# Second attention: running maxima taken off by marker products, and the score products of two batches interleaved by bands

## The reference

```
q, k = apply_rope(split_heads(x)), apply_rope(split_heads((x @ w_dk + b_dk) @ w_uk + b_uk))
v = split_heads((x @ w_dv + b_dv) @ w_uv + b_uv)
attn = softmax(einsum('bhid,bhjd->bhij', q, k) / sqrt(8), axis=-1)
x = layernorm(x + einsum('bhij,bhjd->bhid', attn, v).reshape(Bx, Tx, Dx) @ w_o + b_o)
```

## Time and profile before

| | |
|---|---|
| median of 3 runs | 1437.58 us (1434.99 to 1444.62) |
| the profiled execution's own time | 1433.81 us |
| its span in the profile | 1431.9 us |
| TensorE busy | 1295.6 us, 90% of the span |
| VectorE busy | 957.0 us, 67% |
| ScalarE busy | 863.9 us, 60% |
| second attention (788.4 to 1216.0 us) | 427.6 us |

### The profile page before, as it was taken

One profiled execution on the slowest core, in us unless ns is written; L12 is line 12 of the kernel. 1 busy time (PEld: TensorE's weight loads), 2 busy tenths in 40 slices (PEclk: granted clock), 3 DMA queues, 4 the chain that ended last, 5 costly groups with the idle time before them and its releaser, 6 DMA issues. The chain is left out here.

```text
span 1431.9 us, 33756 instructions
## 1 busy us (share of the span) xinstructions
PE 1295.6 (90%) x10829; PEld 1053.9 (74%) x10829; DVE 957.0 (67%) x2849; ACT 863.9 (60%) x2233; POOL 617.5 (43%) x965
## 2 busy tenths in 40 slices
PE   6999999999999999799997898898889888978877
PEld 5888888888888888799996565555555554756765
DVE  6787877777787887667775667767766753543323
ACT  4777777776777766356643555555554544846643
POOL 3244444444444444435534345444543422435553
PEclk9999999999999999899998679878877975989998
DMA  7020202020312210132131222022050002022215
GB/s 259 20 89 26 86 26 86 30 88 28 97 46 73 83 54 17 55 113 65 57 129 52 76 76 78 21 83 75 22 196 8 13 13 82 18 82 80 78 53 184
DMA packets 56451, 100.88 MB, mean 70 GB/s; under 512 B 11056, under 2 KB 46256, under 8 KB 53616
## 3 DMA queue, kind: packets, MB, share of 16 engines
q1 hardware_dynamic: 46704, 80.06, 17.5%
q0 software_dynamic: 9088, 18.89, 3.8%
q10 hardware_dynamic: 576, 0.86, 0.2%
HBM read 78.81 MB, written 62.06 MB: 98 GB/s over the span
## 5 line engine op out<-in xcount | busy, mean ns | idle before, releaser
L622 ACT ACTIVATE a_prob<-psum,a_nmx 128x128 f32<-128x128 f32 (+1 forms) x512 | 208.3, 425 | 72.8 <-DVE a_nmx L985 72.8
L855 POOL TENSOR_TENSOR a_prob<-a_prob,a_rl 128x128 f32<-128x128 f32 (+1 forms) x256 | 124.3, 507 | 241.7 <-DVE a_rl L989 241.0
L2664 DVE TENSOR_REDUCE f_nmx<-psum 128x4 f32<-128x1024 f32 x120 | 147.0, 1225 | 56.1 <-PE psum L214 52.3
L2418 ACT ACTIVATE a_prob<-psum 128x1024 f32<-128x1024 f32 x128 | 130.9, 1023 | 36.9 <-PE psum L2150 34.0
L629 ACT ACTIVATE a_probt<-psum 128x768 f32<-128x768 f32 x128 | 104.8, 819 | 79.5 <-PE psum L1432 79.5
L902 POOL DMA_INDIRECT yt<-a_yrow,a_dest x78 | 79.4, 1018 | 106.9 <-ACT a_yrow L671 89.4
L622 ACT ACTIVATION_READ_ACCUMULATOR a_prob<-psum,a_nmx 128x1 f32 x512 | 107.9, 211 | 0.0
L1432 PE MATMUL psum<-ident,a_prob 128*128 128x128 f32 x768 | 105.3, 273 | 1.1 <-DVE a_prob L995 0.7
L1789 POOL DMA_INDIRECT yt<-m_yrow,m_dest x78 | 76.1, 975 | 69.7 <-DVE m_yrow L1936 45.7
L974 DVE TENSOR_TENSOR a_qkt<-psum,a_bqk 128x512 f32<-128x512 f32 x128 | 88.2, 689 | 26.3 <-PE psum L109 23.7
L2160 PE MATMUL psum<-a_prob,a_v 128*32 128x256 f32 x1024 | 94.5, 502 | 1.4 <-DVEq L2726 1.3
(11 more groups left out here) (411 smaller groups left out, 3838.6 us busy)
## 6 DMA issues: line engine op xcount, KB each, us to landing
xs<-in_fill SPq DMA_DIRECT2D x144, 264.0 KB, 4.2
a_xrow<-xs SPq DMA_DIRECT2D x39, 132.0 KB
m_xrow<-xs SPq DMA_DIRECT2D x39, 132.0 KB
f_yin<-yt SPq DMA_DIRECT2D x18, 256.0 KB, 2.9
w<-in_w SPq DMA_DIRECT2D x16, 256.0 KB, 3.4
f_yin<-yt SPq DMA_DIRECT2D x7, 512.0 KB, 8.0
f_w<-in_wr SPq DMA_DIRECT2D x2, 1284.0 KB
xs<-in_fill_idle SPq DMA_DIRECT2D x2, 1056.0 KB, 6.3
```

The lines of the kernel that those rows point to most:

```text
L622: last = nc.scalar.activation(prob[:, hp % 4, h, at], S[:, 2 * (hp % 2) + h, at], ACT.Exp, bias=nmx[:, hp % 4, q, h:h + 1], accum_out=lsum ...
L855: last = nc.gpsimd.tensor_tensor(prob[:, hp % 4, 0, at], prob[:, hp % 4, 0, at], rl[:, hp % 4, 0, q:q + 1].to_broadcast(prob[:, hp % 4, 0, ...
L2418: nc.scalar.activation(prob[:, k % 2, 2 * (t % 2):2 * (t % 2) + 2, :], ST[:, 2 * (t % 2):2 * (t % 2) + 2, :], ACT.Exp, scale=SCALE).then_i ...
L2664: nc.vector.reduce_max(f.nmx[:, :, 2 * i:2 * i + 2].rearrange("p q h -> p h q"), R.rearrange("p h (q k) -> p h q k", q=QB), AX.X, negate=T ...
```

## The change

The maxima are no longer added onto the stack. They are split as before, but laid out as 16 high columns and 16 low columns (`f_mh[:, :, 0:32]`, one instruction for each part in place of two), turned by the same two transposes, and copied by ScalarE into a tile of its own, `f_mt` (`turned_maxima`, 128x256). `f_marker` holds for each head h a 128x128 block of which rows h and 16+h are ones. `less_maxima(t)` multiplies it with `f_mt`, the 256 columns taken twice: for each of the two heads one product of all 128 rows with 512 columns, which opens the accumulation in its bank, and onto which the score products of 32 rows are then added (`start=False`). The marker products in `stack` are gone (one of five per group).

Pairs and scores are woven: `pair_and_scores(i, t)` with t = i+1 issues `less_maxima(t)`, waits for the reduction of pair i-1, and then two products of the pair, two of the scores, two of the pair, two of the scores. Since t = i+1 the pair lies in bands 0 and 1 where the scores lie in 2 and 3, or the other way round. Pair 3 comes so with scores 4, behind `outputs(0, p, n)`, and `tail_rows` behind that. On VectorE `maximum(4)` now stands ahead of `route_rows`, and `ranked` behind the last reduction and `split_maxima`.

The diff, cut to its core:

```diff
     f.mh, f.nmx = sb("mh", [P, QB, P], F32R), sb("nmx", [P, QB, H1])
-    f.marks = sb("marks", [P, SELW + 4 * P + T], F32R)
-    f.sel = f.marks[:, 0:SELW].rearrange("p (a k n) -> p a k n", a=4, k=H1 // 4)
-    f.marker = f.marks[:, SELW:SELW + 4 * P].rearrange("p (k n) -> p k n", k=H1 // 4)
-    f.one_row = f.marks[:, SELW + 4 * P:]
+    f.sel, f.marker = sb("sel", [P, 4, H1 // 4, P], F32R), sb("marker", [P, H1, P], F32R)
+    f.pick, f.mt = sb("pick", [P, H1]), sb("mt", [P, T], F32R)
...
             nc.tensor.matmul(out, f.sel[:, 2 * j, k, :], f.qk_h[:, j, :], start=True, stop=False)
-            last = nc.tensor.matmul(out, f.sel[:, 2 * j + 1, k, :], f.qk_l[:, j, :], start=False, stop=j == 0)
-        return nc.tensor.matmul(out, f.marker[:, k, :], f.one_row, start=False, stop=True)
+            last = nc.tensor.matmul(out, f.sel[:, 2 * j + 1, k, :], f.qk_l[:, j, :], start=False, stop=True)
+        return last
...
+    def turned_maxima(n, bank):
+        act.wait_ge(f.mt_ps, n)
+        nc.scalar.activation(f.mt[:], bank[:, 0:T], ACT.Copy).then_inc(f.mt_done, 1)
...
     def split_maxima():
-
-        high, low = (f.mh[:].rearrange("p q (j r) -> p q j r", j=HG)[:, :, :, BAND:LOW].rearrange(
-            "p q j (k c) -> p q j k c", c=2)[:, :, :, :, c] for c in range(2))
-        by_band = f.nmx[:].rearrange("p q (k j) -> p q j k", j=HG)
-        for q in range(QB):
-            last = nc.vector.tensor_copy(high[:, q], by_band[:, q])
-        chain.done(last)
-        for q in range(QB):
-            last = nc.vector.tensor_tensor(low[:, q], by_band[:, q], high[:, q].bitcast(F32), ALU.subtract)
-        last.then_inc(f.nmx_done, 1)
-
-    def add_maxima(p, bank, n):
-
-        dve.wait_ge(f.mt_ps, n)
-        q_rows = f.stk[p][:, :, 0, :]
-        nc.vector.tensor_tensor(q_rows, q_rows.bitcast(F32), bank[:, 0:T].unsqueeze(1).to_broadcast([P, NGR, T]),
-                                ALU.add).then_inc(f.mt_done, 1)
-
-    return (rotate_q_first, rotate_q_rest, rotate_k_first, rotate_k, incoming_variances, incoming_rows, incoming_low, split_maxima,
-            add_maxima)
+        chain.done(nc.vector.tensor_copy(f.mh[:, :, 0:H1], f.nmx[:]))
+        nc.vector.tensor_tensor(f.mh[:, :, H1:2 * H1], f.nmx[:], f.mh[:, :, 0:H1].bitcast(F32), ALU.subtract
+                                ).then_inc(f.nmx_done, 1)
...
                     nc.vector.memset(f.mh[:].bitcast(F32), 0.0)
-                    nc.vector.tensor_copy(f.marks[:, SELW:], sel32[:, SELW:]).then_inc(f.sel_done, 1)
+                    chain.done(nc.vector.tensor_tensor(f.pick[:], g.ident[:, 0:H1], g.ident[:, H1:2 * H1], ALU.add))
+                    nc.vector.tensor_copy(f.marker[:], f.pick[:].unsqueeze(2).to_broadcast([P, H1, P])).then_inc(f.sel_done, 1)
...
-            def pair(i, p):
-
-                for q in range(QB):
-                    for c in range(2):
-                        last = first_scores(2 * i + c, q, p, R[:, c, :])
-                last.then_inc(pair_ps, 1)
-
-            def scores(t, p):
-
-                for k in range(QB):
-                    for h in (2 * t, 2 * t + 1):
-                        rows = slice(LOW * (h % HG), LOW * (h % HG + 1))
-                        last = nc.tensor.matmul(ST[:, 2 * (t % 2) + h % 2, k * T:(k + 1) * T], stk[p][rows, h // HG, 1, k * P:(k + 1) * P],
-                                                stk[p][rows, h // HG, 0, :], start=True, stop=True)
-                last.then_inc(st_ps, 1)
+            def part_of_pair(i, q, p):
+
+                for c in range(2):
+                    last = first_scores(2 * i + c, q, p, R[:, c, :])
+                return last
+
+            def part_of_scores(t, k, p):
+
+                for h in (2 * t, 2 * t + 1):
+                    rows = slice(LOW * (h % HG), LOW * (h % HG + 1))
+                    last = nc.tensor.matmul(ST[:, 2 * (t % 2) + h % 2, k * T:(k + 1) * T], stk[p][rows, h // HG, 1, k * P:(k + 1) * P],
+                                            stk[p][rows, h // HG, 0, :], start=False, stop=k == QB - 1)
+                return last
+
+            def less_maxima(t):
+
+                for h in (2 * t, 2 * t + 1):
+                    nc.tensor.matmul(ST[:, 2 * (t % 2) + h % 2, :], f.marker[:, h, :], f.mt[:].unsqueeze(1).to_broadcast([P, QB, T]),
+                                     start=True, stop=False)
...
-                    def first(i):
+                    def may_pair(i):
+                        if i == 0:
+                            pe.wait_ge(both_act, n * 2 + 2)
+                        elif i == NPR // 2 and turned:
+                            pe.wait_ge(both_act, n * 2 + 3)
+                        else:
+                            pe.wait_ge(pair_done, n * NPR + i)
+
+                    def pair(i):
                         if second:
-                            if i == 0:
-                                pe.wait_ge(both_act, n * 2 + 2)
-                            elif i == NPR // 2 and turned:
-                                pe.wait_ge(both_act, n * 2 + 3)
-                            else:
-                                pe.wait_ge(pair_done, n * NPR + i)
-                            pair(i, 1 - p)
+                            may_pair(i)
+                            part_of_pair(i, 0, 1 - p)
+                            part_of_pair(i, 1, 1 - p).then_inc(pair_ps, 1)
+
+                    def scores(t):
+                        less_maxima(t)
+                        part_of_scores(t, 0, p)
+                        part_of_scores(t, 1, p).then_inc(st_ps, 1)
+
+                    def pair_and_scores(i, t):
+                        pe.wait_ge(exp_done, n * NPR + t - 1)
+                        if not second:
+                            scores(t)
+                            return
+                        less_maxima(t)
+                        may_pair(i)
+                        part_of_pair(i, 0, 1 - p)
+                        part_of_scores(t, 0, p)
+                        part_of_pair(i, 1, 1 - p).then_inc(pair_ps, 1)
+                        part_of_scores(t, 1, p).then_inc(st_ps, 1)
...
-                    scores(0, p)
+                    scores(0)
                     if tail:
                         tail_heads(n + 1, OS)
                     if routed:
                         pe.wait_ge(nt_done, n)
                         pe.wait_ge(osb_done, n * NGR + 1)
-                    first(0)
+                    pair(0)
                     if routed:
                         router(columns_of(n - 2), PV)
                     if tail:
                         pe.wait_ge(o_done, n + 1)
-                    scores(1, p)
-                    first(1)
+                    scores(1)
                     if second:
                         pe.wait_ge(v_done, n + 2)
                     if turned:
                         pe.wait_ge(ksin_done, n + 3)
                     if tail:
                         tail_columns(n + 1, MISC)
-                    pe.wait_ge(exp_done, n * NPR + 1)
-                    scores(2, p)
-                    first(2)
+                    pair_and_scores(1, 2)
                     if tail:
                         tail_project(columns_of(n - 1), n + 1)
-                    pe.wait_ge(exp_done, n * NPR + 2)
-                    scores(3, p)
-                    first(3)
-                    if tail:
-                        pe.wait_ge(rt_done, n + 1)
-                        tail_rows(n + 1)
+                    pair_and_scores(2, 3)
                     if routed:
                         pe.wait_ge(lg_done, n - 1)
                     pe.wait_ge(v_done, n + 1)
                     outputs(0, p, n)
-                    pe.wait_ge(exp_done, n * NPR + 3)
-                    scores(4, p)
+                    pair_and_scores(3, 4)
+                    if tail:
+                        pe.wait_ge(rt_done, n + 1)
+                        tail_rows(n + 1)
                     if routed:
                         pe.wait_ge(osb_done, n * NGR + 2)
                     if turned:
@@ -2305,26 +2313,21 @@
                         router_rows(n - 1, PV)
                     if tail:
                         tail_store(1 - p, n + 1)
-                    pe.wait_ge(exp_done, n * NPR + 4)
-                    scores(5, p)
-                    first(4)
+                    pair_and_scores(4, 5)
                     if routed:
                         pe.wait_ge(lt_done, n - 1)
                     outputs(1, p, n)
-                    pe.wait_ge(exp_done, n * NPR + 5)
-                    scores(6, p)
-                    first(5)
+                    pair_and_scores(5, 6)
                     if fresh:
                         if tail:
                             pe.wait_ge(nt_done, n + 1)
                         incoming(n + 4)
                     outputs(2, p, n)
-                    scores(7, p)
-                    first(6)
+                    pair_and_scores(6, 7)
```

(35 more changed lines are left out.)

5 lines of the change are left out of this document (3 added, 2 removed).

## The result

The changed kernel takes 1477.94 us (median of 4 runs, 1471.48 to 1488.68), the kernel before 1440.07 over the 4 runs beside it: a ratio of 1.0271, 95% interval [1.0198, 1.0345]. It is slower, by 38 us; forecast were 1472 and "slower". The profiled execution of the changed kernel took 1480.05 us, that of the kernel before 1433.81.

A forecast was written before the change was run, and what follows sets the result against it. Bound: second-attention batches, a chain through TensorE and VectorE, 42% at low clock. Full-clock 28.9 plus 1.1 for low clock gives 30.0 against 27.2 us; 14 batches add 38 to 1433.8: 1472, range 1428 to 1502.

The forecast's parts named there:

- The walk: One second-attention batch re-timed in program order at full clock: from 24.4 to 28.9 us, 4.5 us later.
- steps 1 to 9: Successive places in a batch, from pair 1 (+0.8 us) through tail_store and outputs(1) to the next stacks (+4.5 us).
- step 3: Pair 3: outputs(0), 1.0 us, now stands ahead of it, so it starts 1.7 us later.
- a change of kind: TensorE switching between full-row marker and 32-row score products: under 0.1 us each, at most four new a batch.
- the drain rival: Each switch between full-row and 32-row products costs 0.4 us, 1.6 a batch, 22 in all: 1494 us; chance 8%.
- the 0.27 each: Price of TensorE's low clock in second-attention batches before the change: 0.27 us more for each us at it.
- steps 6 and 9: outputs(1) waits for route_rows behind reduction 4 (+3.4 us); last outputs wait for ranked behind reduction 7 (next stacks +4.5).
- Steps 1 and 2: Pair 1 comes 0.8 us later behind marker groups; pair 2, behind the projection and marker 3, 1.5 later.
- small gain for weaving: Pairs woven with scores in other bands: about 0.35 us each for pairs 1 to 3; 4 to 6 have it already.
- Faster: Markers hold the clock at 1.00, worth 2.8 us a batch, if walked delays stay under 2.8: 1416 us; chance 12%.
- The clock stays as it is: Low-clock share unchanged in the second attention: 32.0 us a batch, 4.8 more, 67 in all, 1501 us; chance 12%.
- waits hidden: VectorE reaches reductions earlier, half the 4.5 us goes, clock near 1.00: batch 27.2 us, 1434 us; chance 18%.

The follow-up runs named there:

- a2: Changed kernel plus two dense 128-row by 512-column products in each of its three new TensorE waits, results overwritten: 1458.4 us, ratio 1.0130 to the kernel before.
- e4: Changed kernel with route_rows and ranked back in their old places, and pair 3 and tail_rows ahead of outputs(0) again: 1427.7 us, ratio 0.9927.
- e6: Markers and ScalarE copy in the old unwoven order, with marker groups of scores 2 and 3 moved ahead of pairs 1 and 2: 1407.8 us, ratio 0.9806.
- e3: Changed kernel with both VectorE moves undone (route_rows and ranked back in their old places), the rest kept: 1431.3 us, ratio 0.9957.
- v1: Kernel before with VectorE's two moves alone (route_rows and ranked behind reductions), no markers, no weaving: 1477.6 us, ratio 1.0246.
- e5: Changed kernel with markers and ScalarE copy kept, but nothing woven and all else in the old order: 1409.2 us, ratio 0.9799.
- w1: Kernel before with TensorE's new woven order alone, no markers, VectorE's addition and order kept: 1422.5 us, ratio 0.9887.
- b1: Kernel before with two thrown-away dense 128-row by 512-column products ahead of each of the eight score groups: 1418.1 us, ratio 0.9857.
- b2: Kernel before with four thrown-away dense products a batch, two in each of the waits ahead of pairs 1 and 2: 1407.1 us, ratio 0.9831.

## Why the prediction was right

**The walk.** Counted from scores 0, at full clock; before from the earlier trace rows, forecast, and measured in the changed kernel's batch:

| | before | forecast | measured |
|---|---|---|---|
| pair 1 | 3.65 | 4.2 | 4.52 |
| pair 2 | 5.47 | 6.8 | 6.78 |
| pair 3 | 7.30 | 8.8 | 8.88 |
| `tail_store` | 11.82 | 13.1 | 13.21 |
| `outputs(1)` | 12.74 | 15.9 | 15.94 |
| pair 7 | 18.59 | 21.9 | 22.07 |
| next stacks | 21.16 | 25.5 | 26.43 (with 0.7 of the low clock) |

(Forecast: the times of the prediction less 869.4 for scores 0.) The places of steps 1 to 9 stand. A timeline at full clock, re-walked in program order with the releasers of each wait, was good to 0.3 us at almost every place, and a2's 28.9 us confirms the sum at full clock. Scores 0 came 3.27 behind the first stack product in a2, 2.98 in the batch that was walked: 0.3 later where 0.2 was forecast. One step had the right place for a wrong reason: step 3 put pair 3 late because of `outputs(0)`, but e4 has it at 8.5 without `outputs(0)` ahead of it, since reduction 2 ends only then.

**The sizes that were off.** A marker group took 0.64 (963.68 to 964.32), not the 0.47 of two back-to-back products. I had called a change of kind "under 0.1" and put it at nothing. The 0.17 is not all a change of kind: this group stands behind transposes of all 128 rows, and one that stands behind 32-row products takes 0.67 (993.89 to 994.56 in e6). So the step from 32 rows to 128 is 0.03 by these two, and how the 0.17 is shared between the group and the step back to 32 rows is open. Where a group fell into a wait it was covered. The Trainium skill (TensorEngine Tiling (Array Packing), Key Properties) says that changing the tiling mode drains the engine. The trace does not speak against it, with 0.20 us for a group and both its changes, far below the 0.4 for each change of the drain rival.

**The clock.** Forecast: 12% of the time at the low clock at 0.3 us each, 1.1 us a batch. Measured in the batch shown: 12% (clock 0.94), at 0.44 each, 1.6 us. That batch is one of the better ones: over the eleven from 834.24 to 1173.60 a batch took 30.85 us with 17% at the low clock, so 2.0 us over the 28.9, at 0.38 each; the whole stage had 20% (0.90). The mechanism was right, the share and the price too low. In the kernel before, the low clock also fell on outputs, in the batch at 0.76 from 954.8 to 968.5:

```profile
956.64 1.94 PE L2160 MATMUL psum<-a_prob,a_v 128*32 128x256 f32 x16
...
970.50 0.50 PE L214 MATMUL psum<-a_stk 32*128 32x256 f32 x4 [0.47 <-DVE f_nmx L2664]
```

But there waits stood behind it that shrank: ahead of pair 7 from 1.24 to 0.47, ahead of `tail_store` from 0.42 to nothing. This is 1.2 us of the stretch got back, which fits the 0.27 each. In the changed kernel's batch the low clock came behind the last new wait, on the last outputs and the stacks, with no such wait left.

**Luck in the number.** The forecast added 38 us to a profiled execution, and the medians differ by 38. The two profiled executions differ by 46, which is what the traces have to explain, since the one before was 6 us under its median and the changed one 2 over. By batch, 2.8 us were forecast and 3.3 measured.

**Attribution.** The sum was near, but the steps had unequal weight. The two moved VectorE instructions (steps 6 and 9) are worth 47 us with the rest of the change (e3 against the changed kernel) and 38 by themselves (v1). The markers and the copy in the old order are worth 28 us the other way (e5). TensorE's new order on top of the markers costs 22 (e5 to e3), and without them it gains 14 (w1). So the two moves alone (v1) give the time of the whole change only because the rest of it nearly cancels (e3: 0.9957). Steps 1 and 2 were right about pairs that stand behind marker groups. The prediction's small gain for weaving (0.35 a pair) is neither shown nor refuted, since w1's gain may be the clock's.

**The rivals.** "Faster" named the mechanism that the markers hold the clock. The stage's clock was 0.95 in e5, 0.98 in e6, 0.97 in b1 and 0.91 in b2, against 0.79, and these kernels were 19 to 30 us faster. It was outrun, as its own condition said: the walked delays were 4.5 us a batch against the 2.8 that the clock could give. "The clock stays as it is", "waits hidden" and "drain" are refuted by the stage's 0.90, by the waits' 18.2 and 15.1 us, and by 0.20 for a group with both its changes.

**A version that beats both**: b2 (1407.1), e6 (1407.8) and e5 (1409.2) beat the kernel before by about 2% and are not told apart by these runs.

## What to carry to other kernels

Before moving a small instruction behind a big one on an engine with slack, ask who waits for its signal: `route_rows` (0.17 us) and `ranked` (0.18 us), each set behind a reduction of 1.23 us, cost 38 us in 1440. In this kernel a wait had two prices: its length, which added up over the waits (2.5 us a batch for the two), and the low clock that came with it, which did not. So walk the program at full clock first, then ask on which work the low clock will fall. Dense products put into a wait that exists anyway can pay (b2, a2). Put ahead of work that paces another engine they delay it: with the pairs behind two marker groups e5's gain of 28 us shrank to e3's 6.

## What the runs showed of the hardware

The granted clock fell although TensorE was busy 77% of the stretch before it (2.63 of 3.40 us), and four thrown-away products of 128 rows by 512 columns a batch, put into waits there, made the whole kernel 1.7% faster (b2). Busy time in the records was thus no guide to the clock here. Part of that stretch is groups of four 32-row products, which show 0.50 us each, and part is waits for reductions; which of the two let the clock fall was not tested apart. Products of 32 rows in four different bands ran abreast: eight of them started within 0.23 us (964.32 to 964.55), and eight took 0.44 us until the next work (968.68 to 969.12) where four take 0.43 (874.64 to 875.07). Score products that were only queued together did so as well, in the order of the kernel before, where pair 6 starts at 885.12 and scores 7 beside it:

```profile
885.10 0.38 PE L2150 MATMUL psum<-a_stk 32*128 32x256 f32 x2
...
885.33 0.28 PE L2150 MATMUL psum<-a_stk 32*128 32x256 f32 x2
```

All four products of scores 7 stand ahead of pair 6 in the program, yet by these records its last two started 0.2 us after the pair's first two: products in different bands did not start in program order.
